# Routing with the router stationary, four tiles moving and a ring of eight; the residual sum stored in the choice and slot stages

## The reference, cut to what matters

```
x1   = x + conv[node_row]                  # the residual sum; rows without an edge take a zero row
xn   = (x1 - mean) * rsqrt(var + eps)      # per node, over 512 features
S    = softmax(xn @ W_router + b_router)   # 10000 x 32
G, idx = top_k(S.T, 312)                   # each expert takes the 312 best tokens
y    = scatter_add of G * Expert(xn[idx])
x2   = x1 + y                              # the scatter adds into the stored x1
```

## Time and profile before

| what | value |
|---|---|
| time, median of 3 runs | 3929.25 us (3929.16 to 3936.58) |
| the profiled execution's own time | 3931.07 us |
| its span in the profile | 3929.4 us |
| mean granted TensorE clock | 0.884 |
| busy: PE, PEld, DVE, ACT, POOL | 3238.0, 2735.7, 2492.0, 1346.3, 1235.9 us |
| data moved | 449.57 MB, mean 114 GB/s |
| transfers of `route` per tile | x load, `xn` store, `x1` store, gather: 256 KB each |

### The profile page before, as it was taken

How to read it: one execution, slowest core, us unless ns; L and a number is a source line. 1 busy time by engine, 2 the same in 40 slices (tenths; PEclk the granted TensorE clock), 3 DMA queues, 4 the chain that set the end, 5 groups by cost and what they waited for, 6 DMA issues and landing times. The chain is left out here.

```text
span 3929.4 us, 61612 instructions
## 1 busy us (share of the span) xinstructions
PE 3238.0 (82%) x18274; PEld 2735.7 (70%) x18275; DVE 2492.0 (63%) x5781; ACT 1346.3 (34%) x2520; POOL 1235.9 (31%) x1606
## 2 busy tenths in 40 slices
PE   6845889997774117999999999999779992969999
PEld 1213667776773107999999999999658882857766
DVE  7855877645676874545445444544278886957776
ACT  4633655421111004444444444444211111114443
POOL 4752532223551002232332322322123320025552
PEclk9977999997555558999999999999889995989999
DMA  4313323335993015544444445444221211146663
GB/s 154 101 25 106 106 91 123 102 123 182 302 304 114 0 22 143 143 104 137 140 99 134 117 126 142 106 132 112 50 87 53 59 43 42 64 121 147 158 158 103
DMA packets 250358, 449.57 MB, mean 114 GB/s; under 512 B 65632, under 2 KB 71073, under 8 KB 249591
## 3 DMA queue, kind: packets, MB, share of 16 engines
q1 hardware_dynamic: 176425, 280.66, 21.8%
q0 software_dynamic: 62368, 145.38, 17.0%
q10 hardware_dynamic: 11318, 20.54, 1.4%
HBM read 319.38 MB, written 126.83 MB: 114 GB/s over the span
## 5 line engine op out<-in xcount | busy, mean ns | idle before, releaser
L1432 PE MATMUL experts_psU<-experts_x_hi,experts_up_hi 128*128 128x312 f32 (+1 forms) x1408 | 442.1, 314 | 21.7 <-issue 15.3
L1461 PE MATMUL experts_psY<-experts_hid_hi,experts_dn_hi 128*128 128x312 f32 (+1 forms) x1408 | 439.3, 312 | 0.0
L1433 PE MATMUL experts_psU<-experts_x_lo,experts_up_hi 128*128 128x312 f32 (+1 forms) x1408 | 435.9, 310 | 0.0
L1434 PE MATMUL experts_psU<-experts_x_hi,experts_up_lo 128*128 128x312 f32 (+1 forms) x1408 | 434.8, 309 | 0.0
L1462 PE MATMUL experts_psY<-experts_hid_lo,experts_dn_hi 128*128 128x312 f32 (+1 forms) x1408 | 431.6, 307 | 0.0
L1463 PE MATMUL experts_psY<-experts_hid_hi,experts_dn_lo 128*128 128x312 f32 (+1 forms) x1408 | 430.1, 305 | 0.0
L1391 POOL DMA_INDIRECT experts_xg<-xn,experts_token_i x96 | 123.2, 1283 | 664.3 <-DVE experts_token_i L1558 644.7
L1597 DVE TENSOR_TENSOR experts_hid_lo<-experts_hid,experts_hid_hi 128x312 fp32r<-128x312 f32 (+1 forms) x352 | 161.3, 480 | 250.7 <-ACT experts_hid L1524 250.7
L1522 ACT ACTIVATE experts_hid_hi<-experts_psU,experts_bup 128x312 fp32r<-128x312 f32 (+1 forms) x352 | 183.3, 521 | 319.2 <-PE experts_psU L1434 317.4
L1432 PEld LDWEIGHTS experts_psU<-experts_x_hi,experts_up_hi 128*128 128x128 f32 (+1 forms) x1408 | 264.4, 188 | 23.2 <-issue 20.5
L1589 DVE TENSOR_TENSOR experts_dn_lo<-experts_dn_raw,experts_dn_hi 128x1536 fp32r<-128x1536 f32 (+1 forms) x128 | 207.9, 1624 | 98.3 <-ACT experts_dn_hi L1500 98.2
(11 more groups left out here) (402 smaller groups left out, 8117.8 us busy)
## 6 DMA issues: line engine op xcount, KB each, us to landing
experts_dn_raw<-in_L_ffn_W_down SPq DMA_DIRECT2D x96, 768.0 KB, 4.6
conv<-gcn_diff SPq DMA_DIRECT2D x120, 256.0 KB, 2.9
experts_up_raw<-in_L_ffn_W_up SPq DMA_DIRECT2D x32, 682.5 KB, 8.5
index_xt<-in_x SPq DMA_DIRECT2D x78, 256.0 KB, 2.7
route_xt<-in_x SPq DMA_DIRECT2D x78, 256.0 KB, 5.0
x<-route_xt SPq DMA_DIRECT2D x78, 256.0 KB, 4.5
xn<-route_xn ACTq DMA_DIRECT2D x78, 256.0 KB, 4.7
two_xt<-x SPq DMA_DIRECT2D x78, 256.0 KB, 2.8
```

Of the source, the lines that this page charges most:

```text
L1432: pe.matmul(acc, up_hi[:, c, cols], x_hi[:, c, :], start=(c == 0), stop=False)
L1433: pe.matmul(acc, up_hi[:, c, cols], x_lo[:, c, :], start=False, stop=False)
L1434: mm = pe.matmul(acc, up_lo[:, c, cols], x_hi[:, c, :], start=False, stop=(c == C - 1))
L1461: pe.matmul(acc, dn_hi[0:w, m, cols], hid_hi[0:w, m, :], start=(m == 0), stop=False)
```

## The change

In `route` the ring grows from four to eight buffers. The sum is not stored. ACT normalizes, with the scale `rstd` and a bias `shift`, and POOL gets one more instruction per tile for `shift`; POOL now does `root` for tile t - 3 ahead of the gather. The router's weights become the stationary operand (32 columns) and four tiles move through them at once (512 columns), so the logits come out transposed: DVE adds the bias for four tiles at once, PE turns four tiles back, and DVE copies them into `probs`. The gathers stay plain ones that DVE adds.

The stored sum is made a second time by a new class, `Residual`: SP loads a tile of x into one of eight buffers, POOL gathers the rows with an accumulating transfer on top, and SP stores it to `g.x`, five tiles behind the load. Tiles 0 to 64 are done in `choose`, where SP's loop stands between the two stores of marks; tiles 65 to 78 in `slot_rows`, where POOL's part stands behind its four short instructions. Both stages end with waits on these stores.

```diff
-    D, NT, N, R = g.D, g.NT, g.N, 4
+    D, NT, N, R, Q = g.D, g.NT, g.N, 8, 4
...
             def load(t, j):
                 r = node_rows(g, t)
                 at_least(sp, normed, t, R)
-                sp.sem_inc(waited, 1)
-                landed(sp, stored, t, j, R, 1)
                 sp.dma_start(xt[0:r, j, :], x[bass.ds(t * P, r), :]).then_inc(loaded[j], 16)
...
-            tiles(sp, NT, [(0, load), (2, store)], R)
+            tiles(sp, NT, [(0, load)], R)
...
                 pool.tensor_tensor(rstd[:, j:j + 1], mv[:, j, 2:3], g.minus_half[:, 0:1], ALU.pow).then_inc(rooted, 1)
-            tiles(pool, NT, [(0, gather), (2, root)], R)
+                pool.wait_ge(rooted, t * 2 + 1)
+                pool.sem_inc(waited, 1)
+                pool.tensor_scalar(shift[:, j:j + 1], mv[:, j, 0:1], -1.0, rstd[:, j:j + 1],
+                                   ALU.mult, ALU.mult).then_inc(rooted, 1)
+            tiles(pool, NT, [(3, root), (0, gather)], R)
...
+                k, n = j // Q, size(t, j)
+                pe.wait_ge(copied, t + 1)
...
                 for c in range(C):
-                    mm = pe.matmul(psR[:, j % 2, 0:X], xT[:, j, c * P:(c + 1) * P], wr[:, c, :],
+                    mm = pe.matmul(psR[0:X, k, 0:n * P], wr[:, c, :], xT[:, k, c, 0:n * P],
...
+            def turn_back(t, j):
...
+                for q in range(n):
+                    mm = pe.transpose(psB[:, k, q * X:(q + 1) * X], lT[:, k, q * P:(q + 1) * P], g.ident[0:X, 0:X])
+                mm.then_inc(backed, n)
+            tiles(pe, NT, [(4, turn_back), (0, turn), (1, logits)], R)
...
+                act.activation(xn[:, j, :], xt[:, j, :], ACT.Identity, bias=shift[:, j:j + 1],
+                               scale=rstd[:, j:j + 1]).then_inc(normed, 1)
...
+            tiles(act, NT, [(2, copy), (0, norm)], R)
...
-            tiles(v, NT, [(0, mix), (1, norm), (3, take)], R)
+            tiles(v, NT, [(0, stats), (5, bias), (7, take)], R)
...
+class Residual:
+    R, LAG = 8, 5
...
+    def load_and_store(self, sp):
+        for s in range(self.span.start, self.span.stop + self.LAG):
+            if s in self.span:
+                r, j = node_rows(self.g, s), s % self.R
+                if s - self.R in self.span:
+                    sp.wait_ge(self.stored[j], 16 * self.turn(s - self.R))
+                sp.dma_start(self.keep[0:r, j, :], self.x[s * P:s * P + r, :]).then_inc(self.loaded[j], 16)
+            t = s - self.LAG
+            if t in self.span:
+                r, j = node_rows(self.g, t), t % self.R
+                sp.wait_ge(self.mixed[j], 16 * self.turn(t))
+                sp.dma_start(self.g.x[t * P:t * P + r, :], self.keep[0:r, j, :]).then_inc(self.stored[j], 16)
...
+    def mix(self, pool):
+        for t in self.span:
+            r, j = node_rows(self.g, t), t % self.R
+            pool.wait_ge(self.loaded[j], 16 * self.turn(t))
+            pool.indirect_dma_start(self.keep[0:r, j, :], None, self.g.conv[2],
+                                    bass.IndirectOffsetOnAxis(ap=self.g.node_row[0:r, 1, t:t + 1], axis=0),
+                                    compute_op=ALU.add).then_inc(self.mixed[j], 16)
...
             sp.dma_start(table[:, :, 1, :], turned[:, :, :]).then_inc(stored, 16)
+            residual.load_and_store(sp)
             sp.wait_ge(marks_sb, J // G)
             sp.dma_start(table[:, :, 0, :], marks[:, :, :]).then_inc(stored, 16)
             sp.wait_ge(stored, 32)
+            residual.wait_stored(sp)
...
+                kept = sub.sb("kept", [P, Residual.R, g.D])
+                early = g.NT - 2 * Residual.R + 2
```

More of the change, by code:

```diff
@@ L929, in route @@
         rstd = ph.sb("rstd", [P, R])
+        shift = ph.sb("shift", [P, R])
         most = ph.sb("most", [P, TT])
@@ L997, in logits @@
                                    start=(c == 0), stop=(c == C - 1))
-                mm.then_inc(routed, 1)
-            tiles(pe, NT, [(0, turn), (1, logits)], R)
+                mm.then_inc(routed, n)
+            def turn_back(t, j):
+                if not ends_group(t, j):
+                    return
+                k, n = j // Q, size(t, j)
+                pe.wait_ge(biased, t + 1)
+                if not isinstance(t, int) or t >= R:
+                    pe.wait_ge(taken, group_end(t, j) - R)
+                pe.sem_inc(waited, 1)
+                for q in range(n):
+                    mm = pe.transpose(psB[:, k, q * X:(q + 1) * X], lT[:, k, q * P:(q + 1) * P], g.ident[0:X, 0:X])
+                mm.then_inc(backed, n)
@@ L1005, in copy @@
                 at_least(act, normed, t, 0)
                 act.dma_start(g.xn[bass.ds(t * P, r), :], xn[0:r, j, :]).then_inc(nstored[j], 16)
+            def copy(t, j):
+                q = j % Q
                 at_least(act, turned, t, 0)
-                at_least(act, routed, t, R)
-                act.copy(xT[:, j, :], psT[:, j % 2, :]).then_inc(copied, 1)
-            tiles(act, NT, [(0, copy)], R)
+                if not isinstance(t, int) or t >= R:
+                    act.wait_ge(routed, group_end(t, j) - R)
+                act.copy(xT[:, j // Q, :, q * P:(q + 1) * P],
+                         psT[:, j % 2, :].rearrange("p (c l) -> p c l", c=C)).then_inc(copied, 1)
@@ L1054, in _, with __init__, turn, wait_stored @@
             step(v.memset(probs[:, NT:TT, :], -1.0))
-def choose(nc, g, probs, K, upto_tile, in_tile):
+class Residual:
+    R, LAG = 8, 5
+    def __init__(self, nc, g, x, ph, keep, first, stop):
+        self.g, self.x, self.keep, self.span = g, x, keep, range(first, stop)
+        self.loaded, self.mixed, self.stored = (ph.sems(n, self.R) for n in ("res_loaded", "res_mixed", "res_stored"))
+    def turn(self, t):
+        return (t - self.span.start) // self.R + 1
+    def load_and_store(self, sp):
[10 more added lines that the diff above has]
+                sp.dma_start(self.g.x[t * P:t * P + r, :], self.keep[0:r, j, :]).then_inc(self.stored[j], 16)
+    def wait_stored(self, sp):
+        for t in self.span[-self.R:]:
+            sp.wait_ge(self.stored[t % self.R], 16 * self.turn(t))
+    def mix(self, pool):
[5 more added lines that the diff above has]
+                                    compute_op=ALU.add).then_inc(self.mixed[j], 16)
+def choose(nc, g, probs, K, upto_tile, in_tile, x, kept, early):
     TT, X = probs.shape[1], probs.shape[2]
@@ L1100, in choose, with _ @@
         block = ph.block()
+        residual = Residual(nc, g, x, ph, kept, 0, early)
         assert J % G == 0 and TT * X % 512 == 0
         W = TT * X // 512
+        @block.gpsimd
+        def _(pool):
+            residual.mix(pool)
         @block.tensor
@@ L1238, in _, with slot_rows @@
             init(v.tensor_tensor_scan(em(upto_tile), em(starts), em(in_tile), 0.0, ALU.mult, ALU.add))
-def slot_rows(nc, g, K, upto_tile, in_tile, tile_of, rest, row):
+def slot_rows(nc, g, K, upto_tile, in_tile, tile_of, rest, row, x, kept, early):
     X, TT = upto_tile.shape[1], upto_tile.shape[2]
@@ L1253, in slot_rows, with _ @@
         begun, found_step = ph.sem("begun"), ph.sem("found_step")
+        residual = Residual(nc, g, x, ph, kept, early, g.NT)
         block = ph.block()
+        @block.sync
+        def _(sp):
+            residual.load_and_store(sp)
+            residual.wait_stored(sp)
         @block.gpsimd
@@ L2307, in program @@
                 route(nc, g, x, w["L0_ffn_W_router"], w["L0_ffn_b_router"], probs)
[L2308 to L2309 removed]
+                kept = sub.sb("kept", [P, Residual.R, g.D])
+                early = g.NT - 2 * Residual.R + 2
+                choose(nc, g, probs, K, upto_tile, in_tile, x, kept, early)
+                slot_rows(nc, g, K, upto_tile, in_tile, tile_of, rest, row, x, kept, early)
             experts(nc, g, K, tile_of, rest, row, w["L0_ffn_W_up"], w["L0_ffn_b_up"], w["L0_ffn_W_down"], w["L0_ffn_b_down"])
```

72 lines of the change are left out of this document (42 added, 30 removed).

## The result

The changed kernel takes 3962.06 us (median of 3 runs, 3957.69 to 3966.67) against 3929.25: a ratio of 1.008, 95% interval 1.0066 to 1.0095. It is 0.8% slower, clear of noise and inside the range, but 20 us above the forecast. Its profiled execution has a span of 3959.1 us, 29.7 more than before.

A forecast was written before the change was run, and what follows sets the result against it. The prediction took the DMA engines (share 0.91) to bound `route` before, with POOL next. Route -11.3, choose +14.6 and slots +9.2 gave +12.5 us on the profiled 3931.07, 3943.6, median 1.8 below: 3942 us; range 3912 to 3972.

The forecast's parts named there:

- the size of POOL's turn in the changed kernel: `route`: POOL takes the DMA's place as the bound at 3.20 us a tile, bounds 3.05 and 3.30; route -11.3 us.
- 2.63 + 0.43: `route`: POOL's undisturbed period before, 2.63 us, plus 0.43 for the added `shift`, taken as 3.05 us a tile.
- holds: `route`: disturbance of POOL, 0.11 us a tile for the copies and 0.04 for the gather and the power.
- The eight buffers bring nothing: `route`: the ring of eight brings nothing by itself, costed at nothing.
- the router's shape brings nothing: `route`: the stationary router brings nothing by itself, costed at nothing; PE at 2.9 us a tile stays below POOL.
- The tail: End of `route`, last add to last logits: 13.9 us instead of 9.6, +4.3; at the high clock 2.7 less.
- Choose, +14.6 forecast: `choose`: 65 residual tiles at 2.7 us make the second store of marks late, landing at 1438.5 against 1423.9.
- POOL's held starts: `choose`, last 40 us: DVE's two-input instructions can hold POOL's starts, put at 4 us.
- Rival 2: `choose` and slots: two-input or fast scalar DVE instructions stop POOL, queue not full; 3971 us, slower still; chance 0.13.
- Slots, +9.2 forecast: Slots: the store of the 14 residual tiles lands at 1466.5, against DVE's end at 1457.3.
- Rival 1: Transfers overlap, 2.5 us a tile or less in `choose`, `route` at 3.05 with POOL unheld; 3912 us, faster; chance 0.25.
- Rival 3: Gain and debt cancel: `route` at 3.05 gives -22.6, `choose` +14.6, slots +9.2; 3930.5 us, no change; chance 0.20.

The follow-up runs named there:

- odd_residual_lag3: odd_residual with POOL's power (`root`) one tile later (lag 3 instead of 2) and VectorE's normalization, bias and taking back one tile later too; 3890.00 us, ratio 0.9907.
- r8_alone: The kernel before with a ring of eight instead of four in `route` and nothing else; 3938.89 us, ratio 1.0029.
- r8_pad24: r8_alone with 24 needless transposes on PE behind the last tile of `route`; 3919.74 us, ratio 0.9980.
- store_in_route_dve: The changed kernel with VectorE normalizing as before, no `shift`, the sum stored in `route` again and no residual later; 3920.63 us, ratio 0.9981.
- plain_residual_gather: The changed kernel with the residual's gather overwriting instead of adding, so `x1` lacks the input's rows; 3938.17 us, ratio 1.0028.
- odd_residual: store_in_route_dve, but `route` stores only the even tiles' sum and the residual makes the 39 odd ones in `choose`; 3917.29 us, ratio 0.9974.

## Why the prediction was right, and where not

**What bounds `route`.** The step of the sum that failed is the size of POOL's turn in the changed kernel, 3.20 us forecast and 3.40 measured, so that of a gain of 0.21 us a tile 0.01 was left; its parts are in the next paragraph. That this turn is the bound was right. Behind it stands a misreading of the kernel before. I took the DMA as its bound and a POOL that waits for nobody (2.63 + 0.43) as the next. The earlier trace rows shows such a turn, but in 225 us of the kernel before, 960 to 1185, POOL also waited for the statistics:

```profile
POOL route_rstd L975 <- DVE route_mv L137: 45.0, 45, 2.6
```

I read that as the DMA's shadow. odd_residual_lag3 shows such a wait to be a bound of its own in a `route` with the same lag: a list with too few turns between a gather and the instruction that needs its result. For the kernel before, which has the same list and a ring of four, this is an inference. What is shown there is that 0.91 was not full, by shares of 0.94 to 0.95 in r8_alone, r8_pad24 and store_in_route_dve. In the changed kernel, where the lag is 3, this wait is small (0.12), and the period is that of POOL with its `shift`.

**The period after, 3.20 forecast, 3.40 measured.** The undisturbed turn is 3.12 instead of 3.05. For holds I gave 0.15 and the trace shows some 0.22: the `shift` is held 0.16 on average (417 against 263 ns), the power 0.05 (628 against some 575) and the gather 0.01 (1049 against 1040). The copy isn't held any more (186 ns; the earlier trace rows has 287): the hold passed to the instruction now in its place. The wait for the statistics, 0.12, had no term at all. Together 3.46 where 3.40 was measured, so this sum is good to 0.06; both are outside my bounds of 3.05 and 3.30. Which instruction carries it was right: without the `shift` 3.17.

**"The eight buffers bring nothing"** was wrong, by 0.17 us a tile beside a store in `route`; in the changed kernel it was hidden behind the `shift`. That the router's shape brings nothing was right, also that PE's clock doesn't matter here. The tail was 11.4 us instead of 13.9 (1206.6 to 1218.0), 2.5 less (I had said 2.7 for the high clock): the granted clock was 0.50 up to 1210 and 1.00 from there on, and the last group's matmuls of 384 columns came 0.32 us apart where I had 0.64.

**Choose, +14.6 forecast, +17.3 measured.** The mechanism and its main term held: 2.7 us a tile forecast, 2.68 measured; share 1.05 forecast, 1.08 measured; DMA work 2.90 forecast, and 1.08 x 2.68 = 2.89 measured. Two terms beside it were wrong by 5 to 7 us and nearly cancel, which is luck. The first gather began 7.6 us after the store of the turned marks, where I had 12.5. And I had let the last gather's tile end at the pace of the others, 0.4 us ahead of the second store of marks; that store came 7.2 us after the start of the last gather, at 1426.66, which had to land first and be stored. Between the first and the last gather lie 173.7 us, forecast 173.3. In there are POOL's held starts, for which I took 4 us:

```profile
1387.20 6.28 POOL L1129 DMA_INDIRECT probs_kept<-conv,all_node_row  x1 [0.30 <-issue]
...
1414.18 6.63 POOL L1129 DMA_INDIRECT probs_kept<-conv,all_node_row  x1 [0.30 <-issue]
...
1426.66 1.54 POOL L1129 DMA_INDIRECT probs_kept<-conv,all_node_row  x1 [0.30 <-issue]
```

The thirteen gathers from 1378.39 on lasted 2.98 us on average and came 3.29 us apart instead of 2.68; the last four came 1.85 apart and made up for some of it. From 1378.39 to the last one it is 48.3 us for 16 turns, 5.1 more than at 2.7. Rival 2, with 22 us for the holds, asked too much: a gather is held only where it starts beside such an instruction, 6.28 us beside a scan of 5.49. This agrees with the rule of the Trainium skill (GPSIMD Engine Reference, Key points) that POOL contends with VectorE's instructions of two SBUF inputs. The search's counts held nobody, 1.54 us a gather beside them, and no count became longer than 2.88, as forecast.

**Slots, +9.2 forecast, +11.1 measured**: from the first of its 14 gathers to the last passed 33.5 us where I had 31.6. Three of them were held (4.17, 3.01 and 3.98 us); the gathers landed 6.5 us after their issue, where the earlier trace rows has 4.9. VectorE was done 11.6 us before the barrier (9 forecast).

**The rivals.** Rival 1 needed 2.5 us a tile in `choose`; plain_residual_gather shows that at 2.17 its `choose` would have been right, but the accumulating gather here took 2.68, and its `route` at 3.05 would have failed too. The changed kernel moved 292 GB/s in the search, the run with the plain gather 361. The estimate of 2.2 us a tile from the 358 GB/s of the Trainium skill (DMA: Bandwidth & Descriptors, Where 436 GB/s comes from) is so near the second and too little for the first. Rival 2's 3971 us is nearer to the 3962 measured than my 3942 is, but not by its mechanism: it had the excess in `choose` and slots, and more than half of it is in `route`. Rival 3's debt was nearly right and its gain fails by the same step as the forecast's. The sum: +12.5 forecast, +31.0 measured between the profiled executions (3931.07 and 3962.06). Of the 18.5 us between the two 10.2 are `route`, 2.7 `choose`, 1.9 slots, 2.4 `experts` and what follows, and 1.3 lies outside the span. That the sign was right owes to the debt, which was sized from rows of the same mix of transfers. That the time lies inside the range is in part luck: the account of `route` was wrong, and the range is 60 us wide.

## What to carry to other kernels

Where an in-order list issues a transfer and later an instruction that needs its result, compare the time to landing and reduction with the turns between the two. A wait of the issuing engine in most turns can be a bound of its own, although no engine and no queue is full; here one more turn of lag gave some 27 us where moving half of the stores away had given 3 (store_in_route_dve to odd_residual). A transfer moved into an idle stretch is free for as many tiles as fit before its end, here 39 tiles did and 65 did not; what doesn't fit comes back as delay, 28.5 us here. Before giving an engine "one small instruction more", ask what its period is without waits: 0.4 us on POOL cost 18 us here.

## What the runs showed of the hardware

- An indirect DMA on POOL that starts beside an instruction of VectorE with two inputs in SBUF lasts until 1.35 to 1.43 us after that instruction's end, in eleven such starts at the end of `choose` and in slots: 1387.20 + 6.28 is 1393.48, where the scan ends at 1392.13. (A twelfth, at 1306.33 in the search, lasted until 1.63 us after; the next instruction of VectorE ran by then.) Beside VectorE's instructions with one input in PSUM (`choose_psW`, 1395.03 to 1400.19) it took 1.54 us as if alone. Of two scalar instructions with one input of 128x2560, of 1.59 and 1.55 us, one left it at 1.65 us, and one held it: that at 1303.73 lasted until 1305.59, 1.41 us after the instruction's end at 1304.18. What sets the two apart isn't shown (the first read f32, the second int16, and the first began 0.07 us ahead of the gather, the second 1.10).
- A gather that adds cost the sixteen DMA engines 1.47 us for 256 KB, a plain one 0.80. With plain gathers the core moved 361 GB/s over 110 us:

```profile
DMA packets 18575, 39.76 MB, mean 361 GB/s; under 512 B 2426, under 2 KB 2426, under 8 KB 18571
```

- With a ring of eight the helper writes out more of `route` for every engine (for PE 248 matmuls in its program instead of 120). With it the loop of `experts` was 17 us slower, through a second stop of some 3 us in each of four turns; 24 needless transposes in front took it away.
